# First attention's values in three tiles of 128 tokens, brought to pair order through DRAM, with a new order of calls, in a fused audio tower

## The reference, cut to what matters

```python
h = einsum('bnf,ef->bne', patches(x), W_tok) + b_tok        # 128 clips, 47 tokens of 192 features each
n = layernorm(h)
q, k, v = n @ Wq, n @ Wk, n @ Wv                            # v is what the change touches
s = where(causal, q @ k.T, -inf)
h = h + softmax(s) @ v                                      # first attention, one head, per clip
h = h + ffn(layernorm(h))   # router with top 2 of 8 low-rank experts on q, k, v; attention with 12 heads; projection
```

## Time and profile before

| what | us |
|---|---|
| median of 3 runs | 622.24 |
| lowest of them | 618.33 |
| the profiled execution, its own time | 624.15 |
| its span, from the first to the last instruction | 622.0 |
| PE busy, share of the span | 571.8, 92% |
| DVE, POOL, ACT busy | 484.4, 381.9, 350.5 |
| 16 DMA engines, share of the span in q1 | 69.2% |
| packets in q1 | 72603 |

### The profile page before, as it was taken

One profiled execution on the slowest core, in us unless ns is written; L12 is line 12 of the kernel. 1 busy time (PEld: TensorE's weight loads), 2 busy tenths in 40 slices (PEclk: granted clock), 3 DMA queues, 4 the chain that ended last, 5 costly groups with the idle time before them and its releaser, 6 DMA issues.

```text
span 622.0 us, 20408 instructions
## 1 busy us (share of the span) xinstructions
PE 571.8 (92%) x7707; PEld 513.6 (83%) x7707; DVE 484.4 (78%) x1310; ACT 350.5 (56%) x689; POOL 381.9 (61%) x647
## 2 busy tenths in 40 slices
PE   5598899899999899999999899999999999897684
PEld 5587788798989889898989798898989897785574
DVE  6544485588888879888888687798888889997774
ACT  3646546376666656566656466566666546453431
POOL 9498888777777747767676577567685705121010
PEclk9899999899999989999999899899999999997956
DMA  8975859879796949687978868397969072735621
GB/s 205 214 154 124 164 122 183 175 150 187 139 198 134 186 109 168 151 160 152 191 151 156 186 111 190 99 175 168 175 130 166 8 140 61 135 76 77 115 37 37
DMA packets 72700, 87.96 MB, mean 141 GB/s; under 512 B 24574, under 2 KB 56655, under 8 KB 71067
## 3 DMA queue, kind: packets, MB, share of 16 engines
q1 hardware_dynamic: 72603, 86.66, 69.2%
HBM read 55.26 MB, written 18.37 MB: 118 GB/s over the span
## 4 chain that ended last, share of the span: by engine, by line
PE 75%; DMA 9%; POOL 5%; DVE 4%; issue 3%; SPq 2%; ACT 2%; POOLq 0%; ACTq 0%; DVEq 0%
PE ps_r L1502 24%; PE ps_tok L1494 7%; PE ps_tok L1495 6%; PE ps_tok L1496 6%; PE ps_p L1758 5%; PE ps_s L1745 5%; PE ps_r L1659 4%; PE ps_r L1494 4%; PE ps_r L1496 4%; PE ps_r L1495 4%; POOL xs L794 3%; DMA raw<-x 3%; DMA k<-qk_scratch 2%; PE ps_r L1788 2%; POOL xe L794 2%
## 5 line engine op out<-in xcount | busy, mean ns | idle before, releaser
L794 POOL TENSOR_TENSOR xs<-raw,xs 90x368 f16<-90x368 f32 x188 | 162.7, 891 | 46.4 <-ACT xs L888 46.4
L1494 PE MATMUL ps_tok<-w_tok,xs 128*128 128x192 f16 x576 | 144.8, 251 | 11.6 <-DMA xs<-xe 3.8
L1495 PE MATMUL ps_tok<-w_tok,xs 128*128 128x192 f16 x576 | 143.6, 249 | 1.8 <-issue 1.8
L1496 PE MATMUL ps_tok<-w_tok,xs 128*128 128x192 f16 x576 | 143.7, 250 | 0.0
L1494 PEld LDWEIGHTS ps_tok<-w_tok,xs 128*128 128x128 f16 x576 | 66.0, 115 | 16.5 <-issue 5.9
L888 ACT ACTIVATE p2T<-ps_p 128x552 f16<-128x552 f32 x64 | 40.4, 631 | 63.4 <-PE ps_r L1496 58.4
L888 ACT ACTIVATE xs<-raw 90x736 f16<-90x736 f32 x96 | 75.4, 806 | 0.0
L794 POOL TENSOR_TENSOR xe<-raw,xe 90x368 f16<-90x368 f32 x64 | 55.9, 885 | 21.5 <-ACT xe L888 21.5
L1495 PEld LDWEIGHTS ps_tok<-w_tok,xs 128*128 128x128 f16 x576 | 66.9, 116 | 1.3
L1496 PEld LDWEIGHTS ps_tok<-w_tok,xs 128*128 128x128 f16 x576 | 66.1, 115 | 2.0 <-issue 1.9
L1023 ACT ACTIVATE qk<-ps_r,b_qk 128x368 f16<-128x368 f32 x48 | 27.2, 567 | 57.1 <-PE ps_r L1496 57.1
(11 more groups left out here) (188 smaller groups left out, 1567.2 us busy)
## 6 DMA issues: line engine op xcount, KB each, us to landing
raw<-x SPq DMA_DIRECT2D x32, 1035.0 KB, 8.1
qk_scratch<-qk SPq DMA_DIRECT2D x32, 276.0 KB, 2.8
q<-qk_scratch SPq DMA_DIRECT2D x48, 138.0 KB, 5.4
k<-qk_scratch SPq DMA_DIRECT2D x48, 138.0 KB, 5.5
xs<-xe SPq DMA_DIRECT2D x30, 184.0 KB
v<-v_scratch SPq DMA_DIRECT2D x64, 76.5 KB, 7.3
out<-h2b SPq DMA_DIRECT2D x16, 240.0 KB
v_scratch<-v2s SPq DMA_DIRECT2D x16, 204.0 KB
```

The costliest lines, as they stand in the source:

```text
L794: nc.gpsimd.tensor_tensor(lo, src, hi, ALU.subtract).then_inc(s_lo, 1)
L1494: mm(dst, stat[0], mov[0], start=start, stop=False)
L1495: mm(dst, stat[0], mov[1], start=False, stop=False)
L1496: return mm(dst, stat[1], mov[0], start=False, stop=stop)
```

## The change

`v_` makes three `deep_product`s of 128 tokens, tiles 0 and 1 into bank v0 and tile 2 into bank v1. `v_copy` copies them to a new buffer `v1t` in tile order. Two new calls on SP bring the values to pair order: `v1_to_scratch` writes `v1t` to DRAM (fp32, two DMAs a group, 276 KB), `v1_to_pairs` reads it back to `v1` by pair (two DMAs). `av` waits for that read instead of for the copies. The order of calls of all engines, LAG, MOVED and RING_AT are new, and STEPS is 39.

```diff
-STEPS = 38
+STEPS = 39
...
+        v1t = sb("v1t", [128, 3, D])
...
+                def v1_to_scratch():
+                    g = group(s, "v1_scratch")
+                    if g is not None:
+                        sp.wait_ge(s_v1, g * 2 + 2)
+                        if g > 1:
+                            sp.wait_ge(s_v1p, (g - 1) * 32)
+                        sp.dma_start(v1_scratch[g % 2, 0:256, :].rearrange("(t p) d -> p t d", p=128), v1t[:, 0:2, :]).then_inc(s_v1w, 16)
+                        sp.dma_start(v1_scratch[g % 2, 256:TG, :], v1t[256 - TILES[2]:128, 2, :]).then_inc(s_v1w, 16)
+
+                def v1_to_pairs():
+                    g = group(s, "v1_pairs")
+                    if g is not None:
+                        sp.wait_ge(s_v1w, g * 32 + 32)
+                        if g > 0:
+                            sp.wait_ge(p_av, g * 2)
+                        for rows in (slice(0, EVEN), slice(EVEN, PT_)):
+                            sp.dma_start(v1[rows, :, 0:D], v1_scratch[g % 2].rearrange("(q r) d -> r q d", r=PT_)[rows]).then_inc(s_v1p, 16)
+
+                v2_to_scratch()
+                stack_qk()
+                v1_to_scratch()
+                extra_rows()
                 store()
+                v1_to_pairs()
+                place_v2()
-                load_next(0)
-                place_v2()
                 load_next(1)
                 h_to_pairs()
+                load_next(0)
                 qk_to_scratch()
-                v2_to_scratch()
-                stack_qk()
-                extra_rows()
...
                         if g:
-                            act.wait_ge(p_av, g * 2 - 1 + n)
-                        copy(v1[:, 2 * n:2 * n + 2, 0:D],
-                             bank(f"v{n}")[0:PT_, 0:2 * D].rearrange("p (a c) -> p a c", a=2), 1 / WS).then_inc(s_v1, 1)
+                            act.wait_ge(s_v1w, g * 32)
+                        tiles = CV_TILES[n]
+                        copy(v1t[:, tiles[0]:tiles[-1] + 1, :],
+                             bank(f"v{n}")[:, 0:D * len(tiles)].rearrange("p (a c) -> p a c", c=D), 1 / WS).then_inc(s_v1, 1)
...
-                        for p in (2 * n, 2 * n + 1):
-                            last = deep_product(bank(f"v{n}")[0:PT_, D * (p % 2):D * (p % 2 + 1)],
-                                                lambda n: xnT[:, g % 2, n, pair_tokens(p)], lambda n: w_v1[:, n, :], True, True)
+                        for i, t in enumerate(CV_TILES[n]):
+                            t0 = TILES[t]
+                            last = deep_product(bank(f"v{n}")[:, D * i:D * (i + 1)],
+                                                lambda n: xnT[:, g % 2, n, t0:t0 + 128], lambda n: w_v1[:, n, :], True, True)
...
-                            pe.wait_ge(s_v1, g * 2 + 2)
+                            pe.wait_ge(s_v1p, g * 32 + 32)
```

More of the change, by code:

```diff
@@ L137 @@
-STEPS = 38
-RING_AT = {"av0": 2, "av1": 1, "qk0": 0, "qk1": 2, "cv0": 1, "qk2": 0, "cv1": 2, "ot0": 1, "xt0": 0, "ot1": 2,
-           "pv0": 0, "yt0": 1, "pr0": 2, "yt1": 0, "pr1": 1, "pv1": 0, "xt1": 1, "ga": 2, "g0": 2, "g1": 0,
-           "v0": 1, "pv2": 2, "sc": 0, "v1": 1, "at": 0, "pt": 2, "pv3": 1}
+LAG = {"v2_scratch": (13,), "lateload": (7, 7, 8, 9, 10, 10), "stack_qk": (13,), "v1_scratch": (11,), "extra_rows": (9,),
+    "store": (15,), "v1_pairs": (11,), "place_v2": (13,), "load_next": (7, 8), "h_to_pairs": (10,),
+    "qk_to_scratch": (12,), "ad": (13,), "ln1": (10, 10, 11), "h2b": (14,),
+    "low": (9, 9, 9, 9, 9, 9, 9, 9, 9, 9, 9, 9, 9, 9, 9, 9), "ln2": (12,), "xn2": (12,), "xn2_twin": (12,),
+    "wact": (7, 8, 9, 10, 10, 12, 12, 13), "high": (10, 10, 10, 10, 10, 11, 11, 11), "exp2": (15, 15, 16, 16),
+    "ga_copy": (14,), "v_copy": (13, 13), "g_high": (13, 13), "router_exp": (14,), "p2t_high": (15, 15, 16, 16),
+    "xn_tile": (12, 12, 12), "exp1": (13,), "ad_high": (14,), "p1t": (13,), "xn_twin": (12,), "qk_high": (14, 14, 14),
+    "cv_high": (14, 14), "o2_twin": (16,), "o_high": (16, 16), "x2_high": (13, 13), "xn_high": (12, 12),
+    "norm2": (15, 15, 15, 15), "x2_low": (13, 13), "wdve": (5, 7, 7, 7, 7, 9, 10, 10), "p2t_low": (14, 15, 15, 15),
+    "xn_low": (12, 12), "max2": (14, 14, 14, 15), "fin": (16, 16), "h_tile": (10, 11, 11), "shift": (14, 14, 14, 15),
+    "stats1": (10, 11, 11), "logits": (13,), "g_low": (12, 12), "ranks": (13,), "dispatch": (13,), "max1": (12,),
+    "ad_low": (13,), "h2": (12, 12), "stats2": (12,), "qk_low": (13, 13, 13), "cv_low": (13, 13), "o_low": (15, 15),
[4 rows of a table added]
@@ L167, in audio_tower @@
 def audio_tower(nc, x, tok_W, tok_b, Wq, Wk, Wv, W_qkv, b_qkv, W_gate, b_gate, A, B_lora,
-                W_proj, b_proj, out, scratch, v_scratch):
+                W_proj, b_proj, out, scratch, v_scratch, v1_scratch):
     with ExitStack() as ctx:
@@ L879, in step @@
                 low(6)
+                low(7)
+                ln2()
+                xn2_()
+                xn2_twin()
+                ln1(0)
+                low(8)
+                low(9)
+                low(10)
+                ln1(1)
+                low(11)
+                low(12)
+                low(13)
+                low(14)
+                low(15)
             for s in range(STEPS):
@@ new lines, in step @@
+                high(7)
+                g_high(0)
+                router_exp()
+                p2t(2)
+                g_high(1)
+                exp2(3)
+                xn_tile(0)
+                p2t(3)
+                high(0)
+                exp1()
+                weights(6)
+                ad_high()
+                exp2(0)
+                high(1)
+                p1t()
+                xn_tile(1)
+                high(2)
+                p2t(0)
+                weights(1)
+                xn_tile(2)
@@ L1099, in step @@
+                weights(2)
+                high(3)
+                exp2(1)
+                xn_twin()
+                qk_high(0)
+                cv_high(0)
+                o2_twin()
+                weights(3)
+                qk_high(1)
+                qk_high(2)
+                o_high(0)
+                cv_high(1)
+                o_high(1)
+                weights(4)
+                high(4)
+                x2_high(0)
+                p2t(1)
+                xn_high(0)
                 x2_high(1)
-                p2t(2)
@@ L1427, in fin @@
                                                        op0=ALU.mult, op1=ALU.add).then_inc(s_fin, 1)
+                norm2(0)
+                x2_low(0)
+                weights(1)
+                p2t(1)
+                xn_low(0)
+                x2_low(1)
+                xn_low(1)
+                max2(3)
+                fin(0)
+                h_tile(1)
+                shift(3)
+                stats1(1)
+                weights(5)
+                logits()
+                g_low(0)
+                ranks()
+                p2t(2)
+                dispatch()
+                fin(1)
+                norm2(1)
                 g_low(1)
+                weights(6)
+                weights(0)
                 h_tile(2)
-                weights(1)
-                dispatch()
-                norm2(2)
-                max1()
-                p2t(3)
+                stats1(2)
                 max2(0)
                 shift(0)
-                stats1(2)
+                max1()
+                norm2(2)
+                p2t(3)
+                max2(1)
+                shift(1)
                 weights(7)
+                weights(2)
                 norm2(3)
@@ L1902 @@
     v_scratch = nc.dram_tensor("v_scratch", (2, TG + V_ROWS - NT, 2 * V_RUN), F16, kind="Internal").ap()
-    audio_tower(nc, *args, out, scratch, v_scratch)
+    v1_scratch = nc.dram_tensor("v1_scratch", (2, TG, D), F32, kind="Internal").ap()
+    audio_tower(nc, *args, out, scratch, v_scratch, v1_scratch)
     r = run_bass_kernel_spmd(nc, [arrays], core_ids=[0])
```

267 lines of the change are left out of this document (96 added, 171 removed), and 62 rows, old and new, of tables (LAG, MOVED).

## The result

After: 631.75 us, median of 4 runs (626.60 to 632.97). The kernel before, beside it: 620.29. Ratio 1.0192, 95% interval 1.0140 to 1.0244: slower, by more than it is uncertain, where a gain of 4 us was forecast. A later measurement of the same two kernels gave 625.25 and 617.41, ratio 1.0106 (1.0059 to 1.0153). Medians here are of all runs, ratios and their intervals of the fast runs alone. The loss is 1 to 2%, and it varies; why is part of what follows.

What follows compares the result with a forecast made beforehand. PE was taken to set the middle step, with DVE and DMA next and the ends bound otherwise. Matmuls -6.6, DMA load +1 and tail +1.5 gave -4.1 us, so 622.24 became 618 us; its own range was 612 to 624.

Steps and rivals of the forecast that it cites:

- Matmuls, -6.6: Values' product on PE: 15 matmuls a group instead of 20 save 0.41 us a group, 6.6 us over 16 groups.
- the rest of the reordering: Middle steps: small waits, from DVE's new order freeing banks late, give the gain back; 622 to 625 us, chance 0.15.
- Copies: Values' copies on ACT: smaller shapes save 0.15 us a group, worth nothing because ACT has room.
- Round trip and who waits behind it, 0: Values through DRAM before av(0): 12.1 to 13.9 us, hidden under 14.1 us of PE work; calls queued behind cost nothing.
- The estimate of 2.3 us: Read of 138 KB from scratch: 2.3 us, leaving some 5 us to spare; queue medians of 5.5 and 7.3 spoke against it.
- Rival 1: At av(0) in each middle step PE waits for late values and loses clock; about 650 us, milder 628; chance 0.14.
- DMA load, +1: DMA engines: 276 KB more each way a group lift the 0.82 share to 0.90 by bytes; 0 to 2 us, taken 1.
- rival 3: PE's "issue" stalls in the middle vanish under the new order, 10.8 us less, giving 606 us; chance 0.11.
- Tail, +1.5: Behind the last token product: the last group's values' round trip lacks cover; taken as 1.5 us, bounds -4 and 6.
- Head, 0: Start of the kernel: av of group 0 stands behind group 2's extra rows and two more DMAs; 0 to 3, taken 0.

Runs made afterwards that it cites:

- new_order_tiles: The changed kernel without the DRAM round trip: the 15 values' matmuls copied straight to v1 in the wrong rows; 624.77 us, ratio 1.0112 to the kernel before.
- old_order_round_trip: The kernel before with the three tiles and the write to and read from scratch, keeping its order of calls; 708.91 us in one run, beside 619.7.
- after_again: The changed kernel, not edited further, measured and profiled a second time; 625.25 us over 10 runs, ratio 1.0106 to the kernel before.
- new_chain_short: The changed kernel with g_low(1) ahead of the dispatch on DVE and g_high(0) ahead of high(7) on ACT; 632.24 us, ratio 1.0240 to the kernel before.

## Why the prediction was wrong

*Matmuls, -6.6.* Right as a price (0.42 a step in the old order), wrong as a gain in the new one: 0.25, and the step as a whole rose to 32.85 instead of falling to 32.13. That even the old order turned it into no shorter kernel is open. My step "the rest of the reordering ... can't gain there, and can lose; that is a rival" named the risk and its place, DVE in a new order; I set 0.15 on it and did not walk DVE's list, where the loop through gT and df could have been found. PE's waits in that loop are 0.5 of the 0.73 us a step; the rest is PE's own and not explained.

*Copies.* Nothing, as taken.

*Round trip and who waits behind it, 0.* Right in the middle: nobody waits, and new_order_tiles without it has the same step. The size was wrong on the careful side: 12.1 to 13.9 us were taken where the middle steps of after need 11.2 to 12.0 (of a room of 15.0 to 15.2, taken as 14.1), because the reads land 3.3 to 4.7 us after their issue and not 5.5 to 7.3. So 3.2 to 4.0 us are spare, not 0.2 to 2.0. The estimate of 2.3 us that the prediction set aside was about as near as the medians it preferred. In the Trainium skill, "DMA: Bandwidth & Descriptors", section "Anatomy of one DMA — SWDGE (gpsimd) path", the figure behind that estimate is for transfers issued by GpSimd, and these are issued by SP. And the room was taken as given where it was what the reordering paid for. Rival 1 did not happen in after and did in old_order_round_trip, dear clock included. That the trip costs in the ends, 1.0112 to 1.0192 or 1.0106, is not settled.

*DMA load, +1.* The share rose to 0.88 and 188 GB/s, between unchanged and my 0.90; cost 0 in the middle.

*Stalls (rival 3).* They are gone in every profile of the new order, worth 10 to 11.5 us of the middle (361.1 with the longer steps). I gave this 0.11 and no mechanism. The places of the stalls give one: PE waits there for its next block of code, and in the middle of every profile of the new order the block is in time. So their absence is luck, as far as the prediction goes, and it hid most of what the longer steps and the head cost.

*Tail, +1.5.* Measured +3.1 and -1.8 in two executions: not told apart from nothing.

*Head, 0.* This is the step that failed. "In the head, `av` of group 0 stands behind extra rows of group 2 and two more DMAs; 0 to 3, I take 0" looked at the moved DMAs alone. Measured: +5.2 in after_again and +13.3 in after, where PE's second idle stretch was followed by 1.2 GHz. 4.0 and 5.7 us of these come with the second group, whose extra rows now stand behind a load of x and land at 46.1 instead of 42.3 us while PE idles. I had read that PE and POOL are both busy nearly 90 of 110 us there, and did not ask what each engine's new list leaves PE to run between 38 and 70 us, nor in which order SP issues the load and the rows. The other step that failed is the matmuls' gain, above: -6.6 was taken whole, and the middle steps lost 3.4 instead.

Sum as it came, for the two executions of after against the first of before: 13.3 - 7.2 + 3.1 = 9.2, and 5.2 - 7.2 - 1.8 = -3.8. Yet the medians differ by 7.8 and 11.5 us: both profiled executions of the kernel before (624.15 and 622.62) are 4 us above its medians (617 to 620). Whether fewer of the stalls come in its other executions, so that the middle gained less than 7 us there, no run here tells.

## What to carry to other kernels

Price a reordering like an edit: walk each engine's new list once around a middle step and once through the start, and ask which loop of engines closes last; a shorter product is worth its time only on that loop. When a round trip is hidden by an order, the order is its cost. Where stalls have no releaser in the profile, count the instructions ahead of them: if their places lie a round number apart, as multiples of 256 do here, look at the queue that brings the code. And a wait of PE where the clock is at stake has two prices, so compare several executions before a difference in the head is explained.

## What was not expected of the hardware

PE waits for its own code, in blocks of 256 instructions, for 0.6 to 2.4 us where a block is late; the figures stand in the section on the result.

The clock behind an idle stretch is not a function of the program: with 2.11 and 1.80 us busy of 4, the one execution went on at 0.53 and the other at 1.00. In the Trainium skill, "TensorE: Matmul & The Clock Gate", section "HAM oscillation — how this bites in real kernels", waits in a loop are told to bring the low clock; the middle of old_order_round_trip agrees (2.85 us for 1.31), the two heads show that one and the same gap may or may not.

Small DVE operations took longer in the new order, at unchanged sizes. From 200 to 480 us, before and then after (total, mean ns):

```profile
L1307 DVE TENSOR_TENSOR over<-ahead,beats 128x192 f32<-128x192 f32 x9 | 3.2, 358 | 0.3
...
L1322 DVE TENSOR_TENSOR disp<-disp,pe_r 128x24 f32<-128x24 f32 x8 | 1.5, 182 | 0.3
```

```profile
L1334 DVE TENSOR_TENSOR over<-ahead,beats 128x192 f32<-128x192 f32 x8 | 7.3, 918 | 0.3
...
L1349 DVE TENSOR_TENSOR disp<-disp,pe_r 128x24 f32<-128x24 f32 x8 | 6.3, 785 | 0.3
```

In the new order they fall beside POOL's splits of x. One step of after, DVE and then POOL:

```profile
349.37 0.92 DVE L1334 TENSOR_TENSOR over<-ahead,beats 128x192 f32<-128x192 f32 x1
350.32 0.35 DVE L1336 TENSOR_REDUCE rank<-over 128x24 f32<-128x192 f32 x1
...
351.99 0.79 DVE L1349 TENSOR_TENSOR disp<-disp,pe_r 128x24 f32<-128x24 f32 x1
```

```profile
348.23 4.50 POOL L820 TENSOR_TENSOR xs<-raw,xs 90x368 f16<-90x368 f32 x5
352.86 0.84 POOL L828 TENSOR_TENSOR ad<-ga,disp 128x384 f32<-128x384 f32 x1
```

The two with two operands are longer by 918 - 358 and 785 - 182 ns, the reduction with one operand between them is not. L1349 ends together with the last of POOL's five splits (348.23 + 4.50 = 352.73; 351.99 + 0.79 = 352.78). By the Trainium skill, "SBUF — State Buffer", section "SBUF: two separate sides", a DVE instruction with two SBUF inputs and a GpSimd one that reads SBUF take turns at a shared port, whole instructions at a time; these rows fit it. In new_chain_short L1349 starts behind the last split and takes 183 ns again, and L1347, also with two operands, which starts during it, takes 294 ns instead of 183. L1334 and L1349 together are 1.2 us longer a step, on the chain that now closes the step, and no such row was visible in the kernel before. What the step would be without both was not tried; new_chain_short is without one of them, and its step is 32.73.
